# A state-space layer on one core: product of state 7 on GpSimd in odd images, the last image's order written out, zero matmuls ahead of the first convolution

## What is computed

```python
hs_c = conv1d(hs, conv_w); hs = silu(hs_c + conv_b)
dt_r, Bm, Cm = split(hs @ W_x.T, [R, R + N])
dt = softplus(dt_r @ W_dt.T + b_dt)
A = -exp(A_log)
def step(state, inp):                       # over the positions, N states for each channel
    dA = exp(dt_t[:, :, None] * A)
    state = dA * state + dt_t[:, :, None] * B_t[:, None, :] * u_t[:, :, None]
    y = einsum('bin,bn->bi', state, C_t)
y = (ys + hs * Dp) * silu(gate)
h = x + y @ W_out.T                         # rmsnorm, mean over 4 directions, layernorm follow
```

## Time and profile before

| | |
|---|---|
| median of the runs | 848.98 us |
| the profiled execution | 847.56 us |
| its span, first to last instruction | 845.8 us |
| busy: PE, VectorE, ScalarE, GpSimd | 93%, 93%, 90%, 89% of the span |
| scan of state 0, from one image to the next | 49.82 us |
| first scan of the first image | 36.63 us |
| DMA | 284 GB/s over the span, 240.6 MB |

### The profile page before, as it was taken

The page is one execution under the profiler, slowest core; times in us unless marked ns, Lnnn a source line. Parts: engine busy times, 40 slices in busy tenths (PEclk is TensorE's granted clock), DMA queues, the critical chain, the costliest instruction groups (busy, mean ns, idle before and its releaser), DMA issues.

```text
span 845.8 us, 10516 instructions
## 1 busy us (share of the span) xinstructions
PE 789.4 (93%) x2738; PEld 398.5 (47%) x2738; DVE 787.5 (93%) x537; ACT 759.9 (90%) x1438; POOL 748.6 (89%) x346
## 2 busy tenths in 40 slices
PE   7599999999999999999999999999999999999787
PEld 4335454454544445444454544444454554445343
DVE  2299999999999999999999999999999999999993
ACT  4899999999999999999999999999999999998551
POOL 0499999999989999998999999899999989999980
PEclk7899999999999999999999999999999999999999
DMA  1698999899998898989888898988989899888970
GB/s 46 248 292 295 294 314 300 300 292 307 315 286 308 301 294 284 321 300 310 307 293 293 294 312 305 293 305 309 305 280 312 282 312 312 297 295 293 302 265 6
DMA packets 73706, 240.61 MB, mean 284 GB/s; under 512 B 12848, under 2 KB 16176, under 8 KB 73648
## 3 DMA queue, kind: packets, MB, share of 16 engines
q1 hardware_dynamic: 73648, 239.96, 84.5%
HBM read 236.78 MB, written 3.15 MB: 284 GB/s over the span
## 4 chain that ended last, share of the span: by engine, by line
DMA 23%; ACT 23%; issue 16%; DVE 15%; POOL 13%; PE 8%; SPq 2%; ACTq 0%; DVEq 0%; POOLq 0%
DMA c_all<-bc_dram 13%; ACT scaled L834 10%; DMA b_all<-bc_dram 10%; POOL inp L1006 9%; ACT ps_x L804 6%; DVE state L1136 5%; DVE ps_x L1143 4%; PE ps_y L582 3%; POOL state L1012 3%; DVE state L1150 3%; DVE state L1143 2%; PE ps_w L473 1%; ACT ps_w L721 1%; SPq L343 1%; ACT oln L863 1%
## 5 line engine op out<-in xcount | busy, mean ns | idle before, releaser
L582 PE MATMUL ps_y<-state,packed 128*128 128x512 f32 x1024 | 473.2, 598 | 5.9 <-POOL state L1012 5.8
L1006 POOL TENSOR_TENSOR inp<-du,b_all 128x1024 f32<-128x1024 f32 x192 | 450.4, 2366 | 2.1 <-DMA b_all<-bc_dram 1.9
L1143 DVE TENSOR_TENSOR_SCAN ps_x<-ps_x,inp 128x1024 f32<-128x1024 f32 x144 | 325.6, 2281 | 3.4 <-ACT ps_x L804 3.4
L1012 POOL TENSOR_TENSOR state<-state,c_all 128x1024 f32<-128x1024 f32 x112 | 263.5, 2360 | 36.1 <-DVE state L1136 33.1
L582 PEld LDWEIGHTS ps_y<-state,packed 128*128 128x128 f32 x1024 | 191.4, 191 | 214.4 <-issue 196.9
L804 ACT ACTIVATE ps_x<-step,a_neg 128x1024 f32<-128x1024 f32 x192 | 213.8, 1114 | 43.4 <-DVE state L1150 21.9
L1150 DVE TENSOR_TENSOR state<-ps_x,c_all 128x1024 f32<-128x1024 f32 x144 | 172.2, 1214 | 1.8
L834 ACT ACTIVATE scaled<-dut,bt 128x128 f32<-128x128 f32 x512 | 154.4, 391 | 0.0
L1136 DVE TENSOR_TENSOR_SCAN state<-decay,ps_x 128x1024 f32<-128x1024 f32 x64 | 145.0, 2265 | 9.4 <-PE ps_x L568 9.4
L1143 DVE TENSOR_TENSOR_SCAN state<-ps_x,inp 128x1024 f32<-128x1024 f32 x48 | 109.7, 2285 | 7.5 <-issue 3.5
L568 PE MATMUL ps_x<-packed,scaled 128*128 128x128 f32 x512 | 68.3, 277 | 10.9 <-ACT scaled L834 9.2
(11 more groups left out here) (123 smaller groups left out, 622.2 us busy)
## 6 DMA issues: line engine op xcount, KB each, us to landing
c_all<-bc_dram SPq DMA_DIRECT2D x256, 512.0 KB, 5.9
b_all<-bc_dram SPq DMA_DIRECT2D x192, 512.0 KB, 6.4
bc_dram<-bc_rows SPq DMA_DIRECT2D x64, 32.0 KB, 2.2
xa<-in_x_t SPq DMA_DIRECT2D x16, 64.0 KB, 8.1
out<-ofin SPq DMA_DIRECT2D x16, 64.0 KB, 3.8
packed<-in_packed SPq DMA_DIRECT2D x1, 635.0 KB, 4.1
packed<-in_packed SPq DMA_DIRECT2D x1, 129.0 KB, 2.5
w_qkv<-in_w_qkv SPq DMA_DIRECT2D x1, 64.0 KB, 2.0
```

The source lines that it names most:

```text
L582: last = mm(ps_y[:, HALF * half:HALF * (half + 1)], ident, state[n % H_RING][:, HALF * half:HALF * (half + 1)], start=(n == 0), stop=(n == ...
L1006: tt(inp[i % IN_RING][:, :], du[b.buf][:, :], b_all[i % B_RING][:, :], ALU.mult).then_inc(pool_inputs, 1)
L1012: tt(state[n % H_RING][:, :], state[n % H_RING][:, :], c_all[n % C_RING][:, :], ALU.mult).then_inc(pool_products, 1)
L1143: v.tensor_tensor_scan(held if KIND[n] == "P" else x, x, inp[i % IN_RING][:, :], 0.0, ALU.mult, ALU.add).then_inc(scans, 1)
```

## The change

State 7 becomes kind P in the odd images 1 to 13 (`ODD_KIND`): VectorE's scan writes `state`, GpSimd forms the product. Counts of semaphores that were multiples of a number per image become tables. The orders of all engines are written anew; SP's lists of loads (not shown beyond a few lines) are among them. The last image leaves the loop and has its own order in `finish`. In PE's prologue `warm` calls are added and moved, and the second image's `qkv` goes behind the first convolution.

```diff
 KIND = "ACCPACCCCPACPACC"
+LAST_KIND = "ACCPACCCCPACPACC"
+ODD_KIND = "ACCPACCPCPACPACC"
+KINDS = [ODD_KIND if b % 2 else KIND for b in range(IMAGES - 1)] + [LAST_KIND]
...
# SP, steps
...
                 if coming:
-                    load_b(coming, 3)
+                    load_b(coming, 5)
                     load_c(coming, 0)
-                    load_b(coming, 5)
                     load_c(coming, 1)
                 if done:
                     store_out(done)
+                if coming:
+                    load_b(coming, 6)
...
# PE, prologue
-                warm(6)
+                warm(8)
                 pe.wait_ge(qkv_weights_in, 16)
                 qkv(first)
+                warm(2)
                 pe.wait_ge(attn_weights_in, 16)
                 scores(first)
-                warm(2)
-                warm(2)
+                warm(3)
+                step_weights()
                 attn_turn(first)
                 attn_out(first)
+                warm(4)
                 pe.wait_ge(zeroed, 9)
                 mean_square(first)
-                step_weights()
-                warm(1)
-                qkv(second)
+                warm(7)
                 pe.wait_ge(conv_weights_ready, 1)
                 conv(first, 0)
                 conv(first, 1)
                 pe.wait_ge(weights_ready, 1)
                 gate_proj(first)
+                qkv(second)
                 bc_proj(first)
...
# PE, steps
                 if done:
                     sum_state(done, 13)
+                    sum_state(done, 14)
                 if coming:
                     mean_square(coming)
                 if done:
-                    sum_state(done, 14)
                     sum_state(done, 15)
                     hid_residual(done)
                     hid_proj(done)
+                sum_state(b, 0)
+                if done:
                     hid_mean(done)
-                sum_state(b, 0)
+                sum_state(b, 1)
                 if coming:
                     conv(coming, 0)
                 turn_input(b, 4)
...
-                turn_input(b, 13)
                 if later:
                     scores(later)
+                turn_input(b, 13)
...
# ScalarE, prologue
                 dut_copy(first, 0)
+                dut_copy(first, 1)
+                act_input(first, 0)
+                attn_copy(second)
                 sb_decay(first, 0)
-                dut_copy(first, 1)
-                attn_copy(second)
-                act_input(first, 0)
                 act_input(first, 4)
...
# ScalarE, steps
                 if coming:
                     residual(coming)
                 ps_decay(b, 1)
+                ps_decay(b, 2)
                 if coming:
                     rms_inverse(coming)
-                ps_decay(b, 2)
+                act_input(b, 10)
+                if done:
+                    hid_squares(done)
+                ps_decay(b, 3)
+                if coming:
+                    pad(coming)
+                if done:
+                    hid_inverse(done)
                 sb_decay(b, 4)
-                act_input(b, 10)
-                if done:
-                    hid_squares(done)
-                if coming:
-                    pad(coming)
-                if done:
-                    hid_inverse(done)
-                ps_decay(b, 3)
                 if coming:
                     silu_table(coming)
                     conv_silu(coming, 0)
...
                     exp_table(coming)
+                ps_decay(b, 9)
+                if coming:
                     bc_copy(coming)
-                ps_decay(b, 9)
...
                 ps_decay(b, 15)
+                if coming:
+                    act_input(coming, 4)
                 if later:
                     attn_copy(later)
-                if coming:
-                    act_input(coming, 4)
...
# GpSimd, steps
-                product(b, 3)
+                product(b, 4)
                 scan_input(b, 8)
-                product(b, 4)
                 scan_input(b, 9)
                 scan_input(b, 11)
+                product(b, 7)
                 if coming:
                     scan_weight(coming)
                 scan_input(b, 12)
-                scan_input(b, 14)
                 product(b, 9)
                 product(b, 10)
+                scan_input(b, 14)
+                product(b, 12)
                 scan_input(b, 15)
-                product(b, 12)
+                product(b, 13)
...
                     scan_input(coming, 7)
+                    product(coming, 3)
...
# VectorE, finish: the last image written out
+                done = j + -1
+                product(done, 15)
+                scan(j, 0)
+                scan(j, 1)
+                gated(done)
...
+                scan(j, 5)
+                product(j, 5)
+                scan(j, 6)
+                scan(j, 7)
+                product(j, 6)
+                product(j, 7)
+                hid_norm(done)
+                scan(j, 8)
+                product(j, 8)
+                scan(j, 9)
...
# VectorE, steps
+                if done:
+                    product(done, 15)
                 scan(b, 0)
                 scan(b, 1)
+                if done:
+                    gated(done)
                 if coming:
                     rms(coming)
-                if done:
-                    gated(done)
                 product(b, 1)
...
                 scan(b, 11)
-                product(b, 11)
                 if later:
                     pooling(later)
+                product(b, 11)
                 scan(b, 12)
-                scan(b, 13)
                 if later:
                     row_max(later)
+                scan(b, 13)
...
                 scan(b, 15)
-                product(b, 15)
```

More of the change, by code:

```diff
@@ L35, with numbered, scans_until, before @@
 KIND = "ACCPACCCCPACPACC"
[L36 to L42 removed]
+LAST_KIND = "ACCPACCCCPACPACC"
+ODD_KIND = "ACCPACCPCPACPACC"
+KINDS = [ODD_KIND if b % 2 else KIND for b in range(IMAGES - 1)] + [LAST_KIND]
+def numbered(kinds):
+    return {key: i for i, key in enumerate((b, n) for b in range(IMAGES) for n in range(N) if KINDS[b][n] in kinds)}
+def scans_until(table, index):
+    return next(N * b + n + 1 for (b, n), i in table.items() if i == index) if index >= 0 else 0
+def before(table, num):
+    return sum(1 for b, n in table if b < num)
+POOL_IN, ACT_IN = numbered("CP"), numbered("A")
+DVE_OUT, POOL_OUT = numbered("C"), numbered("AP")
 EXP_LN, SILU, SOFTPLUS = "natural_log_exp_and_others", "silu_and_others", "softplus"
@@ L354, in prologue @@
                 store_bc(first)
+                load_c(first, 0)
                 load_b(first, 1)
@@ L951, in steps @@
                 ps_decay(b, 11)
+                if coming:
+                    dut_copy(coming, 1)
                 ps_decay(b, 12)
@@ L1190, in finish @@
             def finish(j):
+                done = j + -1
+                product(done, 15)
+                scan(j, 0)
+                scan(j, 1)
+                gated(done)
+                product(j, 1)
+                scan(j, 2)
+                product(j, 2)
+                scan(j, 3)
+                scan(j, 4)
+                scan(j, 5)
[8 more added lines that the diff above has]
+                scan(j, 9)
+                out_norm(done)
+                scan(j, 10)
+                scan(j, 11)
+                product(j, 11)
+                scan(j, 12)
+                scan(j, 13)
+                scan(j, 14)
+                product(j, 14)
+                scan(j, 15)
+                product(j, 15)
                 gated(j)
```

213 lines of the change are left out of this document (141 added, 72 removed).

## The result

The changed kernel takes 855.19 us (median of 4 runs, 854.8 to 858.19), the kernel before 849.04 beside it: ratio 1.0088, interval 1.0073 to 1.0103. That is 6.8 us more than the 848.4 I forecast, and 1.2 us past 854, the end of the wider range. The profiled execution took 854.8 us, with a span of 852.7.

What follows compares the result with a forecast made beforehand. VectorE and ScalarE both full between scan 0 and scan 5. Start -2.0, image 0 -0.1, images 1 to 14 +1.8, last image -0.3: -0.6, so 848.4 us on the median's scale; range 845 to 851.5, 8 in 10 839 to 854.

Steps and rivals of the forecast that it cites:

- My own sign of being wrong: Mid-run image: VectorE without gaps and odd images near 48 us, or scan 0 to scan 5 above 17.2, gated product waiting for PE.
- The chain: ScalarE's new order from scan 0 to scan 5: 16.86 us against 16.16, 0.70 more in every image with a coming one.
- Rival 2: Hidden projection becomes late through PE's sum of state 15; at 0.4 us more, 6 us slower, 854; chance 0.15.
- Odd images: Product 7 on GpSimd in seven odd images: VectorE gains, scan 9's decay moves up; 0.9 us less for each.
- Behind scan 5: Pooling now stands between scan 11 and product 11: 0.12 us less per image.
- The start with image 0: PE's clock up for the first convolution: 2.0 us gained at scan 1, plus 0.1 in image 0.
- The last image: Written-out order removes two waits of VectorE, two products follow their scans directly: 0.3 us less, between 0 and 0.8.
- Rival 1: VectorE alone sets the pace, ScalarE's chain not binding: 830.5 us, or 840 if half absorbed; chance 0.18.
- Rival 3: PE's clock stays at 1.2 GHz in the first convolution, so the start gains nothing: 851 us; chance 0.12.
- The loads moved past each other: SP's reordered loads, tightest the load of c for state 0: priced at 0, up to 0.2 us an image.

## Why the prediction was wrong

Much of the mechanism was right: the decay of state 2 waits for scan 0, VectorE waits ahead of the hidden norm and scan 5, the odd product is a gain, and the ScalarE chain in all images outweighs it. What I had wrong is that this chain hangs on scan 0 alone; its second root, PE's sum of state 15, stands in my sum at nothing. My own sign of being wrong came true: scan 0 to scan 5 above 17.2, with the gated product waiting for PE. On the scale of the profiled execution I had -0.6 and the runs show 854.8 - 847.56 = +7.24; the 7.84 between them are these:

- **The chain: +0.70 forecast, 17.33 - 16.16 = +1.17 measured, in 14 images 6.6 us.** This is the step that failed. The missing 0.47 are 0.14 ahead of the squares, 0.30 ahead of the decay of state 3, 0.11 for the SBUF decay of state 4 (1.15 ahead of a table load, where I took 1.04), less 0.08 on the decays of states 2 and 3. I had seen both waits, bounded them at 0.2 together, and found the sum of state 15 "0.1 to 0.2 us late already, which the 2.43 of copies covers". The earlier trace rows speak against that: squares start 2.55 after the copies there (241.62 - 239.07), right after the hidden projection's end (240.32 + 1.25 = 241.57), so a wait of 0.12 stood in them that my sum dropped. I made it a condition that the sum ends "about 4.5 us after scan 0 starts"; it ended at 4.94 in the kernel before and ends at 4.72 now. VectorE wants it 0.4 earlier than it comes, and the copies don't cover the decay of state 3 at all: that follows VectorE's product 1, behind the gated product. Moving this decay forward took away its cover. Rival 2, which I gave 0.15, names this matmul and this size (0.4 us, 854), and the run with the output projection moved shows it by itself: 0.41. Only its title doesn't fit: the hidden projection isn't later than before (squares 6.80 us after scan 0, before 7.03), the new orders need it earlier.
- **Odd images: 0.90 forecast, 0.69 measured**, 1.5 us. The new limit ahead of scan 9 is ScalarE, as I wrote, but I took its time from the earlier trace rows without asking what PE's new order does to the softplus ahead of it; that is the 0.23.
- **Behind scan 5** an even image is 0.07 better than forecast; over 14 images (the odd ones' loss is counted above) 1.0 back. These three make 7.1: images 1 to 14 took 8.91 us more than before, where I had 1.8.
- **The start with image 0: 2.1 forecast, 1.54 measured.** The convolution is within 0.2 of the forecast; scan 1 waits 1.33 us for its decay on ScalarE, 0.95 more than the 0.38 before, where I had allowed 0.8. This is one execution of each kernel; in the eleven profiles with these zero matmuls scan 0 of the first image stands anywhere from 33.81 to 35.61.
- **The last image: 0.3 forecast, 0.40 measured** (46.96 against 47.36), and nothing in the tail. Right. The 0.3 that is left lies around the span, and nothing here explains it.

Rival 1 (VectorE alone, 830.5) was far off: even with the chain short again and GpSimd taking product 7 everywhere the time is 837.3, and GpSimd is the bound there. Rival 3 didn't occur: the first convolution took 3.7 us in each of the eleven profiles that had these zero matmuls. The loads moved past each other cost nothing that can be read, as priced: between 60 and 780 us GpSimd waited for a load twice in the changed kernel, 0.28 and 0.76.

## What to carry over

Where several engines are within a few per cent of full, an image is set by chains across engines, and an order that starts one chain earlier is judged by what it pushes behind the instruction that the others wait for. When an instruction is moved forward, list all that it waits for and price each wait at its new place, also those that its old place hid: here a decay moved past four copies had to wait for a product that had always been done. And a product moved to a slower engine needs room in the orders around it: with the orders of before it cost 0.3% here, with the new ones it gave 0.69 us in each odd image.

## What the runs showed of the hardware

The start differs between executions: with the same zero matmuls the first convolution began anywhere from 15.77 to 17.59 us. The granted clock from 12 to 21 us was 1.00 in seven of these eleven executions and 0.88 to 0.91 in four; in the changed kernel's own it was 0.50 from 12 to 14 us and 1.00 from 15 on, ahead of the convolution at 15.97. Its eight matmuls took 3.67 or 3.68 in all eleven. At the very start the column for the clock says too much: it reads 1.00, but in the kernel before the twelve zero matmuls from 1.05 us on took 2.93 us and eight of the same kind from 6.25 on took 1.06, about half as long each. The low level isn't gone from the start of the changed kernel either: from 34 to 46 us the clock was 0.50 to 0.78 in these eleven, as it was 0.57 in the kernel before, and the sums of the first image run at it. In some images a load of b or c landed so late that GpSimd waited for it, by 0.16 to 1.10 us each time; between 60 and 780 us this came in no image of the kernel before and at most four times in any execution with a profile.
